# First stage of a one-core AdaLN block: matmuls whose products nobody reads, twelve direct fills, and q stored by three transfers

## The chip, the cores and the metric

The kernel runs on one core of a Trainium2 chip. The core has TensorE (PE, with its weight loads shown apart as PEld), VectorE (DVE), ScalarE (ACT), GpSimd (POOL) and SyncE (SP), which here only issues transfers. ACT issues some transfers too. The metric is the device time of one execution in microseconds (us). Every engine works through its own list of instructions in order, and semaphores order the engines among each other.

## The reference

Eight batches of 512 tokens of 128 channels go through a block of attention with 16 heads of 8 channels and a mixture of experts. Weights of the attention are binarized (sign times the row's mean magnitude).

```python
mod = (silu(c) @ wmod).reshape(8, 6, 1, 128)          # sa, ca, ga, sb, cb, gb
h = layernorm(x) * (1 + ca) + sa
q, k, v = (split_heads(binlinear(h, W, b)) for W, b in ((Wq, bq), (Wk, bk), (Wv, bv)))
att = softmax(einsum('bhtd,bhsd->bhts', q, k) * 8 ** -0.5)
y = einsum('bhts,bhsd->bhtd', att, v)
x = x + ga * binlinear(merge(y), Wp, bp)
h = layernorm(x) * (1 + cb) + sb
x = x + gb * (shared_expert(h) + top_2_of_8_experts(h))
```

## The kernel before

**Batches and slots.** Attention goes through the eight batches in turn, and each batch through 16 slots: four groups of four heads, times four tiles of 128 keys. In a slot PE makes four score products (`st`, L1609), ACT takes their exponentials (L868), and PE multiplies them with v (`pv`, L1620). The softmax needs the largest score of each query first. For that, PE makes the scores a second time the other way round into a bank pair (`mx`, L1594), and DVE takes the maxima of the pair (`neg_max`, L1077). One such pair is called a fill: 32 fills a batch, numbered on through all batches, 8 a group of heads, made one after the other into two bank pairs. Fill f may start when the reduction of fill f-2 is over. Eleven fills (0 to 10) are made before the first slot of the first batch; its first five slots make three fills each and later slots two. When a group's eight fills are reduced, PE transposes the maxima (`max_T`, L1527), DVE splits them into two bf16 rows (`split_max`, L1085 and L1087), and two small transfers put them beside q.

**Stacks.** The fills and scores of L1594 and L1609 work on `qs` and `ks`, in which each head's 8 channels stand as three bf16 parts, stacked on 72 rows. The parts come from `first_part` (L429, DVE) and `split_qk` (L437 to L441), go to DRAM (`q_parts`, `k_parts`) and come back as stacks of a group of four heads, three transfers for q and three for k.

**Direct fills.** The first group cannot wait for that. `project_direct` (L1646) projects q and k of four heads onto strips of 32 partitions (into `st` and `pv`), ACT writes them to the space of `x1`, and the fills 0 to 7 are made from these in f32 (L1584). This is what `DIRECT = 1` says.

**Order before the first slot.** It is written out by hand for each engine. On PE: the modulation, the transposes of the normalised x of batch 0 (L1487), the bias on strips (L1637, after all small constants are there), the weights of q and k (L1628), q (L1514), k and q on strips, k, the fills, and between them the weights of v, v (L1520), x of batch 1, its q and its k. DVE does the statistics and normalisation (L1026 to L1034), cleans the weights, and splits q of batch 0 itself; POOL splits k. ACT evacuates all of these, and issues the stores of k, the first two groups of k stacks (L448) and the first maxima's transfers (L928). SP stores q of batch 0 by six transfers (three for the first four heads, three for the others), loads x of batch 2, loads the q stacks of groups 0 and 1, and then waits until group 1 and the first maxima are there before it loads groups 2 and 3.

**After the attention** come the experts (from about 590 us on), which the change leaves as they are.

## Time and profile before

| | us |
|---|---|
| runs of the kernel before | 667.86, 669.41, 663.66; median 667.86 |
| the profiled execution, its time | 667.02 |
| its span, first to last instruction | 665.2 |
| PE busy | 615.2 (92%) |
| DVE busy | 504.9 (76%) |
| ACT busy | 404.1 (61%) |
| POOL busy | 259.2 (39%) |

The busy share is an average. Over most of the attention PE has work all the time; in the first 60 us, where the change is, PE, DVE and ACT take turns in waiting. The granted clock of TensorE is its share of 2.4 GHz: 1.00 is 2.4 GHz, 0.50 is 1.2 GHz.

### The profile page before, as it was taken

The numbers are of one execution on the slowest core, as the hardware profiler recorded it, in microseconds if no ns is written. First come the engines' busy times: TensorE is split into PE (matmuls) and PEld (weight loads), VectorE is DVE, ScalarE is ACT, GpSimd is POOL, SyncE is SP. The second block draws the span as 40 slices with busy tenths as digits, with TensorE's granted clock in tenths as the row PEclk, the third lists the DMA queues.
The fourth block names the chain that finished last, engine by engine and source line by source line (L and its number), as shares of the span: only waits on it lengthen the run. The fifth ranks groups of instructions, "written<-read, shape, count | busy, mean of one in ns | idle before, by whom it ended". The sixth has DMA issues, their size and how long they took to land.

```text
span 665.2 us, 10688 instructions
## 1 busy us (share of the span) xinstructions
PE 615.2 (92%) x3461; PEld 288.7 (43%) x3461; DVE 504.9 (76%) x1065; ACT 404.1 (61%) x791; POOL 259.2 (39%) x309
## 2 busy tenths in 40 slices
PE   4899999999999999999999999999999589886997
PEld 2332324233333333423333333232378578776855
DVE  5779788889988989888998888988467534433567
ACT  2345777777777776777778778678735224433431
POOL 4240041414352451434336235025056656566610
PEclk9969999999999999999999999999999988997999
DMA  3443332442541445344244244214832223222155
GB/s 103 134 121 117 117 114 98 132 131 90 160 123 64 133 134 134 109 149 116 93 147 127 69 133 130 67 50 135 226 81 57 68 65 88 63 68 61 56 185 195
DMA packets 58828, 73.91 MB, mean 111 GB/s; under 512 B 10857, under 2 KB 39819, under 8 KB 58772
## 3 DMA queue, kind: packets, MB, share of 16 engines
q1 hardware_dynamic: 53144, 63.30, 32.0%
q0 software_dynamic: 4320, 8.47, 3.7%
q10 hardware_dynamic: 1308, 1.46, 0.8%
q8 instruction: 28, 0.46, 0.3%
q14 instruction: 28, 0.23, 0.1%
HBM read 38.36 MB, written 34.96 MB: 110 GB/s over the span
## 4 chain that ended last, share of the span: by engine, by line
PE 73%; DVE 12%; ACT 7%; issue 3%; another core or an unknown queue 2%; DMA 1%; SPq 1%; POOL 1%; ACTq 1%; DVEq 0%; POOLq 0%
PE pv L1620 15%; PE st L1609 15%; PE mx L1594 14%; PE mx L1806 7%; DVE neg_max L1077 6%; PE st L1820 5%; PE mx L1754 3%; PE misc L1487 2%; PE misc L1514 2%; PE st L1770 2%; ACT pt L868 2%; PE pv L1794 1%; PE misc L1520 1%; DVE stats_sb L1026 1%
## 5 line engine op out<-in xcount | busy, mean ns | idle before, releaser
L868 ACT ACTIVATE pt<-st 128x512 f32<-128x512 f32 x496 | 282.1, 598 | 105.8 <-PE st L1609 95.9
L1077 DVE TENSOR_REDUCE neg_max<-mx 128x2 f32<-128x1024 f32 x248 | 294.5, 1215 | 47.9 <-PE mx L1594 44.6
L1620 PE MATMUL pv<-pt,vs 128*32 128x512 f32 x1024 | 136.4, 605 | 0.3 <-ACT pt L868 0.3
L745 POOL DMA_INDIRECT routed<-rec,row_u x64 | 64.1, 1002 | 136.6 <-PE pv L1620 114.8
L812 POOL DMA_INDIRECT results<-qs,home_u x71 | 72.0, 1014 | 50.8 <-ACT qs L995 28.4
L1609 PE MATMUL st<-even_qk 74*128 74x512 bf16 x256 | 89.0, 389 | 1.9 <-ACT pt L868 1.1
L1609 PE MATMUL st<-qs,ks 74*128 74x512 bf16 x240 | 81.4, 383 | 1.8 <-ACT pt L868 1.1
L1594 PE MATMUL mx<-ks,qs 72*128 72x512 bf16 x256 | 76.5, 380 | 2.9 <-DVE neg_max L1077 2.5
L1594 PE MATMUL mx<-even_qk 72*128 72x512 bf16 x240 | 74.5, 393 | 4.4 <-DVE neg_max L1077 4.1
L437 POOL TENSOR_TENSOR qk_r<-qk_f,qk_parts 128x512 f32<-128x512 f32 x15 | 17.4, 1161 | 98.8 <-DVE qk_parts L429 98.7
L1609 PEld LDWEIGHTS st<-even_qk 74*128 74x128 bf16 x256 | 20.9, 99 | 71.5 <-ACT pt L868 51.7
L989 ACT ACTIVATE vs<-mx 128x512 f32<-128x512 f32 (+1 forms) x43 | 22.7, 527 | 43.8 <-PE mx L1806 20.9
L1609 PEld LDWEIGHTS st<-qs,ks 74*128 74x128 bf16 x240 | 18.8, 98 | 67.5 <-ACT pt L868 51.5
L1806 PE MATMUL mx<-vs,pt 128*128 128x256 f32 (+1 forms) x224 | 48.1, 361 | 0.0
L1370 DVE TENSOR_TENSOR vs<-vs,mx 128x512 f32<-128x512 f32 (+1 forms) x29 | 17.2, 591 | 36.8 <-ACT vs L989 34.4
L1620 PEld LDWEIGHTS pv<-pt,vs 128*32 128x32 f32 x1024 | 20.1, 108 | 52.9 <-issue 37.6
L995 ACT ACTIVATE qs<-st,ks 128x128 f32<-128x128 f32 x71 | 23.2, 370 | 32.2 <-PE st L1820 20.6
L1806 PEld LDWEIGHTS mx<-vs,pt 128*128 128x128 f32 x224 | 38.8, 208 | 3.4
L1594 PEld LDWEIGHTS mx<-even_qk 72*128 72x128 bf16 x240 | 22.2, 100 | 35.0 <-DVE neg_max L1077 13.0
L1594 PEld LDWEIGHTS mx<-ks,qs 72*128 72x128 bf16 x256 | 23.7, 98 | 31.4 <-DVE neg_max L1077 8.2
L1794 PE MATMUL pv<-ident,ks 128*128 128x128 f32 x71 | 15.7, 287 | 21.9 <-ACT vs L984 13.4
L1370 DVE TENSOR_TENSOR pt<-vs,mx 128x512 f32<-128x512 f32 (+1 forms) x14 | 8.3, 591 | 24.0 <-issue 23.5
(217 smaller groups left out, 798.0 us busy)
## 6 DMA issues: line engine op xcount, KB each, us to landing
routed<-pad_rows SPq DMA_DIRECT2D x64, 260.0 KB
even_qk<-q_parts SPq DMA_DIRECT2D x48, 96.0 KB
qs<-q_parts SPq DMA_DIRECT2D x48, 96.0 KB
ks<-k_parts SPq DMA_DIRECT2D x48, 96.0 KB
even_qk<-k_parts SPq DMA_DIRECT2D x42, 96.0 KB
ks<-routed SPq DMA_DIRECT2D x28, 130.0 KB
q_parts<-qk_parts SPq DMA_DIRECT2D x21, 128.0 KB
k_parts<-qk_parts SPq DMA_DIRECT2D x7, 384.0 KB, 2.3
```

Of the source, the lines that this page charges most:

```text
L745: pool.indirect_dma_start(out=routed_dram, out_offset=bass.IndirectOffsetOnAxis(ap=row_u[:, k, t:t + 1], axis=0), in_=rec[b.par][:, k, t, ...
L812: pool.indirect_dma_start(out=result_dram, out_offset=bass.IndirectOffsetOnAxis(ap=home_u[:, slot, h:h + 1], axis=0), in_=y_u[slot][:, h, ...
L868: act.activation(pt[n % 2][:, hh, :], score_bank(b, n, hh), ACT.Exp, scale=SCALE).then_inc(exp_done, 1)
L989: act.activation(silu_u[u % 2][:, 0:halves(u) * I], up_bank(u, 0), ACT.Silu).then_inc(silu_ready, 1)
L995: last = act.activation(y_u[u % RING][:, h, :], y_bank(u)[:, h, :], ACT.Copy, scale=xu[u % RING][:, h, C:C + 1])
L1077: dve.tensor_reduce(neg_max[g % 2][:, hh, 2 * half:2 * half + 2], mx_bank[half][:], AX_X, ALU.max, negate=True).then_inc(mx_free, 1)
L1370: dve.tensor_tensor(act_u[u % ARING][:, 0:halves(u) * I], silu_u[u % 2][:, 0:halves(u) * I], up_bank(u, 1), ALU.mult).then_inc(act_ready, 1)
L1594: last = pe.matmul(mx_bank[half][:, t, :], qs[b.par][0:PROD, h, q0:q0 + P], ks[b.par][0:PROD, h, :], start=True, stop=True)
L1609: pe.matmul(score_bank(b, n, hh), ks[b.par][0:STACK, h, j * P:(j + 1) * P], qs[b.par][0:STACK, h, :], start=True, stop=True).then_inc(st_f ...
L1620: last = pe.matmul(pv_bank[32 * hh:32 * (hh + 1), :], vs[b.par][:, j, HG * g + hh, :], pt[n % 2][:, hh, :], start=(n % Y_SLOTS == 0), stop ...
L1806: last = pe.matmul(up_bank(u, m // IC)[:, m % IC * rows:(m % IC + 1) * rows], w_unit[u % WRING][:, m * P:(m + 1) * P], xuT[u % 2][:, 0:row ...
L1820: last = pe.matmul(y_bank(u)[:, h, :], act_u[u % ARING][:, first:first + P], w_unit[u % WRING][:, 2 * I + j * C:2 * I + (j + 1) * C], star ...
```

## The change

1. **Unread products.** `keep_busy(n)` issues n matmuls of 128x512 in bf16 from a block of ones into `mx` bank pair 1; nobody reads the result. There are 20 of them on PE ahead of the first strips: 7 at the start, then 5, 4, 2 and 2 between the real steps. DVE sets the ones (one memset).
2. **Loads at the start.** bq and bk come right after Wq and Wk, and have a semaphore of their own, on which the bias on strips now waits; bv, bp, the router's bias and the shared weights come after x of batch 1, whose load is issued as soon as x of batch 0 is normalised.
3. **Twelve direct fills.** The second group of heads is put on strips too (`DIRECT = 2`), and fills 8 to 11 are made from these.
4. **Order.** k and q on strips now stand ahead of q and k. DVE takes k's first part after fill 0, and does no split any more; POOL splits q and k of batch 0, and its constants come after that. The normalisation of batch 1 stands behind the maxima of the first group, and with it batch 1's transposes, q and k on PE. ACT stores k after v is evacuated, issues only the first group's k stack, and issues the first maxima's transfers ahead of batch 1's evacuations; the ones for the k stacks are loaded later.
5. **q stored by three transfers** for all 16 heads; the q and k stacks of groups 1, 2 and 3 follow on SP with no wait for the first maxima, and x of batch 2 is loaded behind group 2.

```diff
-DIRECT = 1
-DIRECT_FILLS = DIRECT * 2 * HG
+DIRECT = 2
+DIRECT_FILLS = 3 * HG
...
+        busy_ops = scratch[1][:, 0:T // 2]
...
-            load_x(B1)
             sp.wait_ge(parts_ready, 1)
-            store_q_heads(0, HG, first_stored[0])
-            store_q_heads(HG, H, q_stored)
-            load_x(B1.plus(1))
-            sp.wait_ge(first_stored[0], 16 * PARTS)
+            store_q_heads(0, H, q_stored)
             load_q_stack(B0, 0)
-            load_q_stack(B0, 1)
-            sp.wait_ge(stack_loaded[0][1], STACK_DMAS)
-            sp.wait_ge(m_row_loaded[0], ROW_DMAS)
-            for g in (2, 3):
+            for g in (1, 2, 3):
                 load_stack(B0, g)
+                if g == 2:
+                    load_x(B1.plus(1))
...
             first_part(dve, B0, 0, use(AHEAD, "q_0"))
-            split_qk(dve, B0, 0)
+            maxima(range(1))
+            first_part(dve, B0, 1, use(AHEAD, "k_0"))
+
+            maxima(range(1, 2 * HG))
+            split_max(B0, 0, use(AHEAD, "m0"))
             layer_norm1(B1)
-            first_part(dve, B0, 1, use(AHEAD, "k_0"))
-
-            maxima(range(DIRECT_FILLS))
-            split_max(B0, 0, use(AHEAD, "m0"))
-            maxima(range(DIRECT_FILLS, FIRST_FILLS))
+            maxima(range(2 * HG, FIRST_FILLS))
...
+            def keep_busy(count):
+
+                ones = busy_ops.bitcast(BF16)
+                for _ in range(count):
+                    pe.matmul(mx_bank[1][:, 1, :], ones[:, 0:P], ones, start=True, stop=True)
+
+            pe.wait_ge(busy_ready, 1)
+            keep_busy(7)
...
+            keep_busy(4)
             ln1_T(B0, use(AHEAD, "ln1_0"))
             spread_bias()
+            keep_busy(2)
             weights_T(0)
-            pe.wait_ge(first_done, 2)
+            keep_busy(2)
+            free(use(AHEAD, "q_0"))
+            project_direct(1, 0, 2)
+            project_direct(0, 0, 2)
             project(0, use(AHEAD, "q_0"))
-            project_direct(1, 0, 1)
-            project_direct(0, 0, 2)
             project(1, use(AHEAD, "k_0"))
...
                 if fill == 5:
+                    project_direct(1, 1, 4)
+                    project_direct(0, 1, 4)
+                if fill == 2 * HG - 1:
+                    max_T(B0, 0, use(AHEAD, "m0"))
+                if fill == 2 * HG:
                     ln1_T(B1, use(AHEAD, "ln1_1"))
-                if fill == DIRECT_FILLS - 1:
+                if fill == 2 * HG + 1:
                     project(0, use(AHEAD, "q_1"))
-                    max_T(B0, 0, use(AHEAD, "m0"))
             project(1, use(AHEAD, "k_1"))
```

**PE, from batch 0's transposes to the first fill, before** (a name's number is that of its bank; x1 is the space of the strips):

```order
L1487 MATMUL misc<-ident,ln1 128x128 x4
L1637 MATMUL st1<-bias_qkv,ident 32x2 x4
L1628 MATMUL st0<-ident,w_nat 128x128 x2
L1514 MATMUL misc<-hT,wT 128x512
L1646 MATMUL st1<-hT,wT 32x512 x4
L1646 MATMUL pv<-hT,wT 32x512 x4
L1514 MATMUL misc<-hT,wT 128x512
L1584 MATMUL mx0<-x1 128x512 x2
```

The same stretch of PE after, with the unread products at L1504:

```order
L1504 MATMUL mx1<-pt1 128x512 x4
L1492 MATMUL misc<-ident,ln1 128x128 x4
L1651 MATMUL st1<-bias_qkv,ident 32x2 x8
L1504 MATMUL mx1<-pt1 128x512 x2
L1642 MATMUL st0<-ident,w_nat 128x128 x2
L1504 MATMUL mx1<-pt1 128x512 x2
L1660 MATMUL st1<-hT,wT 32x512 x4
L1660 MATMUL pv<-hT,wT 32x512 x4
L1528 MATMUL misc<-hT,wT 128x512 x2
L1598 MATMUL mx0<-x1 128x512 x2
```

The strips (32x512) moved ahead of the projection of q, and k's projection follows q's at once; eight unread products stand between the real steps.

PE from fill 7 to the first scores, before; L1487 of batch 1 stands ahead of this piece, between the fills 5 and 6:

```order
L1584 MATMUL mx1<-x1 128x512 x2
L1514 MATMUL misc<-hT,wT 128x512
L1527 MATMUL misc<-ident,neg_max0 16x128
L1594 MATMUL mx0<-even_qk 128x512 x2
L1594 MATMUL mx1<-even_qk 128x512 x2
L1594 MATMUL mx0<-even_qk 128x512 x2
L1514 MATMUL misc<-hT,wT 128x512
L1609 MATMUL st0<-even_qk 128x512
```

PE from fill 5 to the first scores, after (L1660 is the second group's strips, L1541 the transpose of the maxima):

```order
L1598 MATMUL mx1<-x1 128x512 x2
L1660 MATMUL st1<-hT,wT 32x512 x4
L1660 MATMUL pv<-hT,wT 32x512 x4
L1598 MATMUL mx0<-x1 128x512 x2
L1598 MATMUL mx1<-x1 128x512 x2
L1541 MATMUL misc<-ident,neg_max0 16x128
L1598 MATMUL mx0<-x1 128x512 x2
L1492 MATMUL misc<-ident,ln1 128x128 x4
L1598 MATMUL mx1<-x1 128x512 x2
L1528 MATMUL misc<-hT,wT 128x512
L1598 MATMUL mx0<-x1 128x512 x2
L1528 MATMUL misc<-hT,wT 128x512
```

All of batch 1's first work (L1492, L1528) now stands behind the transpose of the maxima, and so behind the reduction of fill 7, and the fills 8 to 10 are f32 fills of the strips in place of bf16 fills of the stacks.

DVE from q's first part to fill 10, before (L1074 and L1077 are the reductions):

```order
L429 CAST qk_parts<-qk_f 128x512
L437 TENSOR_TENSOR qk_r<-qk_f,qk_parts 128x512
L439 CAST qk_parts<-qk_r 128x512
L441 TENSOR_TENSOR qk_parts<-qk_r,qk_parts 128x512
L1034 TENSOR_SCALAR ln<-x_in,mv,rstd 128x128 x4
L429 CAST qk_parts<-qk_f 128x512
L1074 TENSOR_REDUCE neg_max<-mx 128x2 x8
L1085 CAST m_rows<-misc 16x128
L1087 TENSOR_TENSOR m_rows<-misc,m_rows 16x128
L1077 TENSOR_REDUCE neg_max<-mx 128x2 x3
```

The same stretch after:

```order
L432 CAST qk_parts<-qk_f 128x512
L1078 TENSOR_REDUCE neg_max<-mx 128x2
L432 CAST qk_parts<-qk_f 128x512
L1078 TENSOR_REDUCE neg_max<-mx 128x2 x7
L1089 CAST m_rows<-misc 16x128
L1091 TENSOR_TENSOR m_rows<-misc,m_rows 16x128
L1038 TENSOR_SCALAR ln<-x_in,mv,rstd 128x128 x4
```

The three split instructions went to POOL, k's first part now stands behind fill 0, and the normalisation moved from ahead of the fills to behind the split of the maxima, ahead of fill 8.

## Rows read from the trace of the kernel before

**Rows 1.** Head of the page.
```profile
span 665.2 us, 10688 instructions
```
**Rows 2.** Windows: stretch, length, engines' busy time, PEclk (granted clock), DMA share, GB/s.
```profile
17.40:27.00 9.60, 9.49 (x46) 4.15 (x44) 7.38 (x10) 4.03 (x7) 4.87 (x6) 1.00 0.49 146
27.00:31.00 4.00, 2.76 (x10) 0.60 (x6) 3.08 (x3) 0.78 (x1) 0.00 (x0) 1.00 0.70 192
31.00:37.40 6.40, 5.16 (x10) 1.48 (x10) 4.13 (x5) 0.69 (x1) 0.00 (x0) 0.50 0.09 21
37.40:44.70 7.30, 7.30 (x23) 3.70 (x21) 4.16 (x5) 3.88 (x8) 3.31 (x4) 0.50 0.52 153
44.70:60.00 15.30, 13.98 (x69) 3.50 (x71) 14.05 (x24) 9.11 (x17) 3.89 (x5) 1.00 0.47 143
...
601.40:604.70 3.30, 3.30 (x17) 3.30 (x18) 1.77 (x6) 1.41 (x6) 2.60 (x3) 0.53 0.18 56
```
**Rows 3.** Timeline of PE: start us, length us, line, form, count, [idle before, releaser].
```profile
10.45 0.28 PE L1637 MATMUL st<-bias_qkv,ident 128*32 128x2 f32 x8 [1.17 <-DMA router_bias<-L_ffn_routing_bias]
...
11.83 2.08 PE L1514 MATMUL misc<-hT,wT 128*128 128x512 f32 x2 [0.47 <-ACT wT L893]
13.83 1.94 PE L1646 MATMUL st<-hT,wT 128*32 128x512 f32 x8
...
17.40 1.12 PE L1514 MATMUL misc<-hT,wT 128*128 128x512 f32 x2
18.46 1.99 PE L1584 MATMUL mx<-x 32*128 32x512 f32 x8
...
23.11 1.16 PE L1520 MATMUL misc<-wT,hT 128*128 128x128 f32 x8
...
30.15 1.23 PE L1514 MATMUL misc<-hT,wT 128*128 128x512 f32 x2 [1.24 <-ACT hT L845]
...
37.40 1.06 PE L1609 MATMUL st<-even_qk 74*128 74x512 bf16 x2
...
41.67 1.92 PE L1520 MATMUL misc<-wT,hT 128*128 128x128 f32 x8
```
**Rows 4.** Timeline of DVE, the same columns.
```profile
16.97 1.11 DVE L1034 TENSOR_SCALAR ln<-x_in,mv,rstd 128x128 f32<-128x128 f32 x4
19.29 0.43 DVE L429 CAST qk_parts<-qk_f 128x512 bf16<-128x512 f32 x1 [1.20 <-ACT qk_f L853]
19.63 4.81 DVE L1074 TENSOR_REDUCE neg_max<-mx 128x2 f32<-128x1024 f32 x4
25.37 4.86 DVE L1074 TENSOR_REDUCE neg_max<-mx 128x2 f32<-128x1024 f32 x4 [0.92 <-PE mx L1584]
32.58 0.28 DVE L1085 CAST m_rows<-misc 16x128 bf16<-16x128 f32 x1 [2.35 <-PE misc L1527]
...
33.58 3.58 DVE L1077 TENSOR_REDUCE neg_max<-mx 128x2 f32<-128x1024 f32 x3 [0.42 <-PE mx L1594]
39.35 1.22 DVE L1077 TENSOR_REDUCE neg_max<-mx 128x2 f32<-128x1024 f32 x1 [2.19 <-PE mx L1594]
...
45.10 1.22 DVE L1077 TENSOR_REDUCE neg_max<-mx 128x2 f32<-128x1024 f32 x1 [1.59 <-PE mx L1594]
```
**Rows 5.** Timeline of ACT, and the transfers that it issues (ACTq).
```profile
25.69 3.58 ACTq L448 DMA_DIRECT2D even_qk<-k_parts  x6
29.32 0.78 ACT L845 ACTIVATE hT<-misc,mod_T 128x512 f32<-128x512 f32 x1 [4.27 <-issue]
```
**Rows 6.** Timeline of SP's issues: a q stack of one group, and batch 1's q store.
```profile
39.63 2.20 SPq L525 DMA_DIRECT2D even_qk<-q_parts  x3
...
44.29 2.01 SPq L508 DMA_DIRECT2D q_parts<-qk_parts  x3
```
**Rows 7.** Timeline of POOL: the first and the last of k's three split instructions.
```profile
19.79 1.15 POOL L437 TENSOR_TENSOR qk_r<-qk_f,qk_parts 128x512 f32<-128x512 f32 x1 [4.10 <-DVE qk_parts L429]
...
21.81 1.15 POOL L441 TENSOR_TENSOR qk_parts<-qk_r,qk_parts 128x512 bf16<-128x512 f32 x1
```

More of the change, by code:

```diff
@@ L213, in adaln_block @@
         strips_ready = sem("strips_ready")
-        first_stored = [sem(f"first_stored{i}") for i in range(2)]
+        busy_ready = sem("busy_ready")
+        first_stored = sem("first_stored")
         small_loaded = sem("small_loaded")
+        qk_bias_loaded = sem("qk_bias_loaded")
         c_loaded = sem("c_loaded")
@@ L425, in first_part @@
                 dve.wait_ge((q_stored, k_stored)[i], all_stored(b.plus(-1), i))
-            if b.const == 1:
-                dve.wait_ge(first_stored[i], 16 * (PARTS, 1)[i])
+            if b.const == 1 and i == 1:
+                dve.wait_ge(first_stored, 16)
             dve.wait_ge(misc_free, done + 1)
@@ L443, in load_k_stack @@
         def load_k_stack(eng, b, g):
-            eng.wait_ge(*((first_stored[1], 16) if b.const == 0 and g == 0 else (k_stored, all_stored(b, 1))))
+            eng.wait_ge(*((first_stored, 16) if b.const == 0 and g == 0 else (k_stored, all_stored(b, 1))))
             for j in range(PARTS):
@@ L769, in scatter @@
                     scatter_rows(b, i)
+            split_qk(pool, B0, 0)
+            split_qk(pool, B0, 1)
+            rstd(mv1, ve1, var1_ready, rstd1, rstd1_ready, stats1_ready, B1)
+            pool.affine_select(out=earlier_token[:], in_=ones_bf[:], compare_op=ALU.is_gt, fill=0.0, base=0,
+                               pattern=[[1, P]], channel_multiplier=-1).then_inc(consts_ready, 1)
+            pool.memset(marks[:], 0.0).then_inc(consts_ready, 1)
+            pool.sem_inc(rows_free, 2)
+            pool.iota(expert_no[:], pattern=[[1, E]], base=0, channel_multiplier=0,
+                      allow_small_or_imprecise_dtypes=True).then_inc(consts_ready, 1)
+            pool.iota(next_row[0][:], pattern=[[REGION, E]], base=0, channel_multiplier=0,
+                      allow_small_or_imprecise_dtypes=True).then_inc(consts_ready, 1)
+            for k in range(RING):
+                pool.memset(digit[:, k:k + 1], float(E ** k)).then_inc(consts_ready, 1)
+            pool.memset(pad_rows[:], 0.0).then_inc(pad_ready, 1)
+            pool.wait_ge(pad_ready, 1)
+            pool.memset(pad_rows[:, :, C + 1], float(FAR)).then_inc(pad_ready, 1)
+            pool.iota(first_row[:], pattern=[[REGION, E]], base=0, channel_multiplier=0,
+                      allow_small_or_imprecise_dtypes=True).then_inc(consts_ready, 1)
+            pool.iota(unit_start[:], pattern=[[P, 2 * EARLY_PAIRS]], base=0, channel_multiplier=0,
+                      allow_small_or_imprecise_dtypes=True).then_inc(consts_ready, 1)
+            pool.affine_select(out=earlier[:], in_=ones_bf[:, 0:E * E].rearrange("p (e f) -> p e f", e=E), compare_op=ALU.is_gt,
+                               fill=0.0, base=0, pattern=[[1, E], [-1, E]], channel_multiplier=0).then_inc(consts_ready, 1)
+            pool.iota(home[:], pattern=[[TOKENS, K_TOP], [1, TT]], base=0, channel_multiplier=TT,
+                      allow_small_or_imprecise_dtypes=True).then_inc(setup_pool, 1)
             pool.wait_ge(setup_pool, 4)
-            rstd(mv1, ve1, var1_ready, rstd1, rstd1_ready, stats1_ready, B1)
-            split_qk(pool, B0, 1)
             fill_values(pool, 1)
@@ L828, in _ @@
             act.dma_start(wmod_sb[:], wmod).then_inc(wmod_loaded, 16)
-            act.wait_ge(setup_pool, 3)
-            for i in range(2):
-                load_ones(act, i)
             act.wait_ge(misc_full, use(AHEAD, "c") + 1)
@@ L1587, in max_scores @@
                     return
-                if hh == 0 and half == 0:
+                if hh == 0 and half == 0 or fill == DIRECT_FILLS:
                     pe.wait_ge(stack_loaded[b.par][g], STACK_DMAS * (b.half + 1))
```

70 lines of the change are left out of this document (29 added, 41 removed).

## The prediction

> **What bounds the kernel now.** I read the head of the page first, then the windows of the first 60 us, then the timelines of PE and DVE there, and last ACT, SP and POOL. The span is 665.2 us [rows 1], of an execution of 667.02 us; the median of the runs is 667.86. From 44.7 us on PE is busy 13.98 of 15.30 us and DVE 14.05 [rows 2]: from there the kernel is a full line that the change does not touch. So what counts is how much earlier that line starts. As its marker I take the end of fill 14's reduction, 45.10 + 1.22 = 46.32 us [rows 4]: it closes the last long wait of DVE, and every later fill, slot and batch follows it.
>
> Up to the marker DVE does 15 reductions of 1.2 us, and waits between them: 0.92 us ahead of fill 4, 2.35 ahead of the split of the maxima, then 0.42, 2.19 and 1.59 [rows 4]. PE runs at half clock twice. Until about 17.4 us a 512-column f32 projection takes 2.08 us, and at 17.40 it takes 1.12 [rows 3] (the clock column reads 1.00 there, since nothing is recorded ahead of its first change; the durations tell). After 31.0 us the granted clock is 0.50, that is 1.2 GHz, up to 44.7 [rows 2]. Ahead of that fall PE idled 1.24 us [rows 3] and was busy only 2.76 of 4 us [rows 2]. The idling came from ACT, which issued six transfers for 3.58 us before it evacuated batch 1's transposes [rows 5].
>
> **The start.** The bias on strips waited 1.17 us for the last small constant [rows 3], and that wait goes, since bq and bk come early. The unread products keep PE busy from about 1 us, so that the real work from 9 us on should be at 2.4 GHz. The eight behind batch 0's modulation are in its path, but at some 0.27 us each (two bf16 products of 512 columns take 1.06 us at 1.2 GHz [rows 3], so half of half of that at full clock), 2.1 us in all, they fit in while DVE normalises x and cleans the weights; at half clock they would cost up to 2 us of their own. I put the first strip at 10.9 us, where PE's first projection was at 11.83.
> From there, warm: k's and q's strips 0.95 each (half of 1.94), q's projection 1.1, ACT's three evacuations at 0.78 or less [rows 5] ending at 14.65, k's projection to 15.8, fill 0 another 1.0 (half of 1.99 for two) [rows 3]. Fill 0's reduction starts at 16.95, where it was 19.63 [rows 4]: **2.7 us earlier**.
>
> **Fills 1 to 7.** DVE drops q's split, but takes k's first part (0.43) behind fill 0. Fill 3, v (1.16) and fills 4 and 5 fill PE up to 23.9; then come the second group's strips, 2 x 0.95 us of new PE work ahead of fill 6. DVE must wait for fill 4 (0.9 us) and for fill 6 (1.4 us). Fill 7 is reduced at 29.35, where it was 30.23: of the 2.7 us only **0.9** are left.
>
> **Fills 8 to 10 and batch 1.** The transpose of the maxima stands ahead of fill 8, so PE idles from 27.8 to 29.4; then fill 8, and PE idles again, 30.8 to 31.6, while DVE splits the maxima (0.6) and normalises batch 1 (1.11) [rows 4]. Behind that PE has batch 1's transposes, fill 9, q, fill 10, k without a break. Everything now hangs on the clock there.
> Warm: transposes 0.6, fill 1.0, q 1.1, fill 1.0, k 1.1 bring the first score to 36.4 us (it was 37.40). Slot 0 then has three fills, the first f32, and v (1.16); DVE does two first parts (0.75); the chain of reductions 11 to 14 ends at 43.55: **-2.8 us** at the marker.
> With the clock lost at about 30.5 and back at about 36.5: fill 9 takes 1.75 and q 1.7, the rest as before; first score 38.3, marker 45.4: **-0.9 us**.
> With the clock lost and not back: fills 9, 10 and 11 take 1.75 each, q, k and v 1.7 to 1.9 [rows 3]; first score 39.55, marker 49.45: **+3.1 us**. The f32 fills cost here: at half clock each takes 1.75 us (twice a warm one, less its overlap), where the two bf16 products that it replaces take at most 1.06 [rows 3].
>
> **Which of the three.** The row of before has a fall after one gap of 1.24 us beside work that left PE idle 1.24 of 4 us. I forecast gaps of 1.6 and 0.8 in the same 4 us, so I expect the fall. As to the return: before, it took up to 44.7 us, the last 7.3 of them with PE busy all the time [rows 2], of mostly bf16 products on 72 rows; but at the start it came in 5.6 us of f32 work (11.83 to 17.40), and late in the kernel a stretch of f32 work from 601.40 was back at full clock by 604.70 [rows 2, 3]. What stands behind 31.6 us is all f32, so I take 5 us.
> The Trainium skill (TensorE: Matmul & The Clock Gate, HAM oscillation) puts the loss of the clock down to waits of PE that outlast a whole window of its monitor, and my gaps would not do that: by that rule the warm sum of -2.8 holds. This case's trace does not agree, since the clock fell beside a gap of 1.24 us.
>
> **Edits that cost nothing.** POOL splits q before k: q from 15.2, k from 18.6, at 3.2 us each (19.79 to 22.96) [rows 7], so q's parts are there at 18.4 and k's at 21.8 (22.96 before). q's store issues 2.0 us, each q stack 2.2 [rows 6]; with 3 us assumed for a landing, which no row here gives, group 0's stack is there at about 28, and group 0's k stack, issued by ACT behind the second strips at 26.6, at 31: over 5 us ahead of the first score. Uncovered, each would cost its lateness one to one. The first maxima's two transfers go out at 30.4 and have 6 us, but now run beside the stacks of groups 2 and 3, which before waited for them; below nothing I see no gain, above I allow 1 us. x of batch 2 is now loaded at some 33 us and used in slot 1, past 41. Batch 1's evacuation waited 4.27 us behind ACT's issues [rows 5] and no longer does; that gain is already spent, since batch 1's x is normalised later than it was evacuated.
>
> **The rivals.**
> 1. *The clock falls and comes back* near 36.5: -0.9 us, 666.96. Chance 0.46.
> 2. *The clock holds* through both gaps (the rule above): -2.8 us, 665.1. For it: DVE's reductions may start earlier than I have them, and the gaps shrink. Against: the fall of before. Chance 0.25.
> 3. *Slower: f32 fills at half clock.* The clock falls near 30 us and is not back when slot 0's v is projected: +3.1 us, 671.0. It decides from a return later than about 40 us on. Slots of 72-row products without f32 work speak for it, five f32 steps in a row against it. Chance 0.13.
> 4. *The unread products do not raise the clock* ahead of the strips: then k's and q's strips and q's projection take 5.0 us in place of 3.0, and the first reduction starts at about 19.05; 2.1 us are missing all the way, +1.2 us, 669.1. For it: the products are followed by waits for loads and the normalisation. Chance 0.07.
> 5. *Something larger*: all of DVE's waits before the marker (0.92 + 2.35 + 0.42 + 2.19 + 1.59, 7.5 us in all) vanish, which with the start 2.7 earlier, less the normalisation and first part that now stand among them (1.5), would be -8.7 us; or a stack or the maxima land late. Chance 0.09, about evenly.
>
> **How the numbers follow.** The likeliest gives 667.86 - 0.9 = 667.0. Its own range is 665.5 to 669. Rivals 2, 3 and 4 lie at 665.1, 671.0 and 669.1; the runs of before lie up to 4 us from each other's median, so I take 662.0 to 670.8. A change of 1% (6.7 us) is about what a measurement of this kernel can tell from none. Only rival 5 reaches that on the fast side, with 0.06 to 0.07, and on the slow side it and a bad case of rival 3, with 0.05: faster 0.07, same 0.88, slower 0.05.
>
> **What would show it.** In the changed profile: the first strip near 10.9 us, with an f32 projection of 1.1 us from the start (step 1; 2.1 us means rival 4); the first reduction near 17 us; fill 7's near 28.2; two gaps of PE between 27.8 and 31.6; first score between 36.4 and 39.6; fill 14's reduction over by 43.6, 45.4 or 49.5 for rivals 2, 1 and 3, with the granted clock of 28 to 45 us to tell them apart. The difference of this marker should be the difference of the times. If the marker moves by one amount and the span by another, the step that is wrong is that the line behind it is full. If PE waits for a DMA at the first score, the covers were wrong.

## The result and the profile after

The changed kernel takes 674.01 us (median of 11 runs, 667.0 to 676.1) and the kernel before 665.49 (11 runs, 663.3 to 669.4): a ratio of 1.0099, with a 95% interval of 1.0064 to 1.0135. It is **slower by 1.0%**. I had forecast 667.0 and a range of 662.0 to 670.8, with 0.05 on slower by over 1%. The profiled execution took 674.29 us.

The head of its page, of which the first line answers [rows 1]: the span, the busy time of PE, and the granted clock in 40 slices.

```profile
span 672.5 us, 10793 instructions
PE 630.4 (94%) x3513; PEld 293.9 (44%) x3513; DVE 502.3 (75%) x1063; ACT 405.9 (60%) x793; POOL 261.8 (39%) x312
PEclk9659999999999999999999999999999978997999
```

The span is 7.3 us longer, and PE is busy 15 us more (it was 615.2): 20 unread products and the second group's strips were added, and, as the next rows show, more of its work ran at half clock. In the clock row two slices near the start are low (6 and 5). The windows of the first 60 us, in the columns of [rows 2]:

```profile
12.00:17.00 5.00, 4.22 (x17) 1.38 (x14) 1.27 (x2) 2.29 (x4) 2.33 (x3) 1.00 0.05 16
17.00:19.00 2.00, 1.47 (x6) 0.40 (x6) 2.00 (x4) 1.60 (x2) 1.64 (x2) 1.00 0.08 18
19.00:29.00 10.00, 9.94 (x32) 3.99 (x36) 4.81 (x5) 1.24 (x5) 7.03 (x26) 0.51 0.49 141
29.00:33.00 4.00, 2.86 (x16) 0.68 (x8) 1.95 (x2) 1.27 (x2) 0.00 (x0) 0.93 0.63 169
33.00:37.00 4.00, 3.44 (x11) 1.40 (x11) 3.00 (x8) 0.00 (x0) 0.00 (x0) 0.50 0.58 128
37.00:44.80 7.80, 7.80 (x12) 2.07 (x13) 2.66 (x3) 1.46 (x2) 0.00 (x0) 0.50 0.38 110
44.80:53.30 8.50, 8.50 (x24) 3.78 (x23) 4.16 (x5) 3.81 (x8) 3.34 (x4) 0.50 0.00 1
53.30:60.00 6.70, 5.69 (x30) 1.35 (x28) 6.23 (x15) 4.16 (x8) 3.87 (x5) 1.00 0.37 120
```

The clock is lost **twice**: from about 19.2 to 29.3 us, and from 32.8 to 53.3. That is 30.6 us recorded at 1.2 GHz, where before it was 13.7 (31.0 to 44.7), besides the stretch up to 17.4 us that only the durations of [rows 3] give away. From 37 to 53.3 PE works without a break, 16.3 of 16.3 us, and stays at half clock.

PE's timeline (start, duration, line, operation and count, and in brackets the idle time ahead), to be read against [rows 3]. Line numbers have moved: L1598 is L1584 of before (f32 fills), L1660 is L1646 (strips), L1528 is L1514, L1534 is L1520 (v), L1541 is L1527, L1623 is L1609 (scores).

```profile
10.17 1.06 PE L1660 MATMUL st<-hT,wT 128*32 128x512 f32 x8
12.03 1.12 PE L1528 MATMUL misc<-hT,wT 128*128 128x512 f32 x2
17.44 1.13 PE L1598 MATMUL mx<-x 32*128 32x512 f32 x4
19.06 2.00 PE L1598 MATMUL mx<-x 32*128 32x512 f32 x4 [0.49 <-DVE neg_max L1078]
20.99 2.08 PE L1534 MATMUL misc<-wT,hT 128*128 128x128 f32 x8
23.00 3.79 PE L1598 MATMUL mx<-x 32*128 32x512 f32 x8
26.71 1.94 PE L1660 MATMUL st<-hT,wT 128*32 128x512 f32 x8
...
33.56 0.37 PE L1541 MATMUL misc<-ident,neg_max 128*16 128x128 f32 x1 [1.69 <-DVE neg_max L1078]
33.86 2.08 PE L1598 MATMUL mx<-x 32*128 32x512 f32 x4
...
38.92 2.08 PE L1528 MATMUL misc<-hT,wT 128*128 128x512 f32 x2
...
44.80 1.06 PE L1623 MATMUL st<-even_qk 74*128 74x512 bf16 x2
```

The start is as forecast: strips at 10.17, a projection in 1.12 us. But a fill that took 1.13 us at 17.44 takes 2.00 at 19.06, behind a gap of only 0.49 (PE had been busy 5.69 of the 7 us before 19.00). Up to 29 us the f32 work then takes about twice its time. The second gap (1.69 us) is the forecast one, and behind it each f32 fill and projection occupies 2.0 us (38.92 less the start of the fill before it, 36.91). The first score starts at 44.80; it was 37.40.

DVE's timeline, against [rows 4] (L1078 is L1074 of before, L1081 is L1077):

```profile
16.16 1.23 DVE L1078 TENSOR_REDUCE neg_max<-mx 128x2 f32<-128x1024 f32 x1 [1.82 <-PE mx L1598]
...
25.12 1.23 DVE L1078 TENSOR_REDUCE neg_max<-mx 128x2 f32<-128x1024 f32 x1 [2.79 <-PE mx L1598]
...
31.05 2.36 DVE L1078 TENSOR_REDUCE neg_max<-mx 128x2 f32<-128x1024 f32 x2 [3.00 <-PE mx L1598]
...
47.92 1.23 DVE L1078 TENSOR_REDUCE neg_max<-mx 128x2 f32<-128x1024 f32 x1 [3.64 <-PE mx L1598]
...
53.73 1.22 DVE L1081 TENSOR_REDUCE neg_max<-mx 128x2 f32<-128x1024 f32 x1 [1.66 <-PE mx L1608]
```

The last row is fill 14's reduction: **the marker is at 54.95**, 8.6 us later than 46.32. The waits are all for PE, none for a transfer. That the line behind the marker is full, as the prediction held, is seen in the last exponentials of the attention, on ACT's timeline of before and then of after:

```profile
475.13 1.08 ACT L868 ACTIVATE pt<-st 128x512 f32<-128x512 f32 x2
```

```profile
483.53 1.09 ACT L868 ACTIVATE pt<-st 128x512 f32<-128x512 f32 x2
```

From marker to here are 428.8 us before and 428.6 after. The attention ends 8.4 us later; the experts gave back 1.1 of it in this execution, which leaves the 7.3 of the span.

### The profile page after: what moved, and what is told of

It is laid out like the page before. It is cut to its first block, busy times and chain, and to the rows that moved or that the text cites. A ratio compares the mean times of both kernels' runs of the same rounds, so it can differ in the third digit from the quotient of the medians.

```text
span 672.5 us, 10793 instructions
## 1 busy us (share of the span) xinstructions
PE 630.4 (94%) x3513; PEld 293.9 (44%) x3513; DVE 502.3 (75%) x1063; ACT 405.9 (60%) x793; POOL 261.8 (39%) x312
## 4 chain that ended last, share of the span: by engine, by line
PE 75%; DVE 11%; ACT 6%; another core or an unknown queue 3%; issue 2%; DMA 1%; POOL 0%; ACTq 0%; DVEq 0%; POOLq 0%
PE pv L1634 15%; PE st L1623 15%; PE mx L1608 13%; PE mx L1827 7%; DVE neg_max L1081 6%; PE st L1841 5%; PE misc L1492 3%; PE mx L1775 3%; PE misc L1528 2%; PE mx L1598 2%; PE st L1791 2%; ACT pt L868 2%; PE misc L1534 2%; PE pv L1815 1%
## 5 line engine op out<-in xcount | busy, mean ns | idle before, releaser
L1081 DVE TENSOR_REDUCE neg_max<-mx 128x2 f32<-128x1024 f32 x244 | 289.7, 1215 | 45.8 <-PE mx L1608 43.1
L1623 PE MATMUL st<-even_qk 74*128 74x512 bf16 x256 | 89.0, 389 | 1.9 <-ACT pt L868 1.1
L1623 PE MATMUL st<-qs,ks 74*128 74x512 bf16 x240 | 81.4, 383 | 1.8 <-ACT pt L868 1.1
L1608 PE MATMUL mx<-even_qk 72*128 72x512 bf16 x232 | 70.5, 385 | 3.9 <-DVE neg_max L1081 3.6
L1623 PEld LDWEIGHTS st<-even_qk 74*128 74x128 bf16 x256 | 20.9, 99 | 72.6 <-ACT pt L868 51.3
L1623 PEld LDWEIGHTS st<-qs,ks 74*128 74x128 bf16 x240 | 18.8, 98 | 67.5 <-ACT pt L868 51.5
L1078 DVE TENSOR_REDUCE neg_max<-mx 128x2 f32<-128x1024 f32 x12 | 14.5, 1223 | 17.7 <-PE mx L1598 17.7
```

What stands on the lines that cost most here:

```text
L1081: dve.tensor_reduce(neg_max[g % 2][:, hh, 2 * half:2 * half + 2], mx_bank[half][:], AX_X, ALU.max, negate=True).then_inc(mx_free, 1)
L1608: last = pe.matmul(mx_bank[half][:, t, :], qs[b.par][0:PROD, h, q0:q0 + P], ks[b.par][0:PROD, h, :], start=True, stop=True)
L1623: pe.matmul(score_bank(b, n, hh), ks[b.par][0:STACK, h, j * P:(j + 1) * P], qs[b.par][0:STACK, h, :], start=True, stop=True).then_inc(st_f ...
```

## The experiments

All went by the same two marks, marker and last exponentials, and by a ratio to the kernel before on the same chip. The chips differ (the kernel before takes 642 us on two of them, 666 and 669 on others), so only ratios are compared. I give them with the 95% interval. Marker and last exponentials are of one execution of each kernel, the profiled one; the ratio is of all its runs, and the two need not match one for one. Every run also has its mean granted clock, and where the runs of one kernel differ in it I say so.

| kernel | marker | last exponentials | ratio |
|---|---|---|---|
| before | 46.32 | 475.13 | 1 |
| changed | 54.95 | 483.53 | 1.0099 [1.0064, 1.0135] |
| a_nobusy | 52.14 | 484.31 | 1.0149 [1.0116, 1.0183] |
| d_first_hold | 49.94 | 478.47 | 1.0075 [1.0038, 1.0113] |
| d_second_hold | 47.46 | 476.49 | 0.9986 [0.9957, 1.0016] |
| a_fillers | 42.84 | 471.85 | 0.9968 [0.9954, 0.9981] |
| a_direct1 | 45.83 | 474.68 | 1.0019 [0.9997, 1.0041] |
| d_direct1_fillers | 45.14 | 474.78 | 1.0014 [0.9996, 1.0033] |
| a_early | 46.61 | 486.89 | 1.0017 [0.9967, 1.0068] |
| a_early_fillers | 46.97 | 477.85 | 1.0002 [0.9970, 1.0033] |
| b_busy | 43.92 | 473.25 | 0.9974 [0.9954, 0.9994] |
| b_stores | 49.90 | 478.45 | 1.0044 [1.0018, 1.0069] |
| b_stores_fillers | 47.64 | 476.63 | 1.0008 [0.9989, 1.0028] |
| b_fillers | 42.23 | 471.15 | 0.9934 [0.9908, 0.9961] |
| b_busy_fillers | 46.56 | 475.82 | 0.9936 [0.9910, 0.9963] |
| b_fill_dense | 42.51 | 471.89 | 0.9966 [0.9945, 0.9988] |
| c_dense | 40.73 | 469.32 | 0.9913 [0.9886, 0.9940] |

Names with a_ and d_ are made from the changed kernel, b_ and c_ from the one before. "Products" below are unread ones, as in part 1 of the change.

**Does the order lose, or the clock?** a_fillers is the changed kernel with thirteen more products, at the two places where its clock falls.

```diff
+                if fill == 2:
+                    keep_busy(4, pv_bank)
                 if fill == 2 * HG - 1:
+                    keep_busy(6, st_bank[0])
                     max_T(B0, 0, use(AHEAD, "m0"))
                 if fill == 2 * HG:
+                    keep_busy(3, st_bank[0])
                     ln1_T(B1, use(AHEAD, "ln1_1"))
```

> The changed kernel with 13 more unread products in TensorE's waits: 4 behind fill 2, 6 ahead of the transpose of the maxima, 3 ahead of batch 1's transposes; at full clock 2.8 us of work, placed where TensorE stood still. Theory C (half clock is the loss): the clock holds or comes back soon, the fill 14 reduction ends at 43 to 45 us in place of 54.95 (before: 46.32), the time is 0.993 to 0.998 of before. Rival O (the order is the loss: second group's strips, f32 fills, batch 1's work behind the maxima, whatever the clock): the clock holds and the time is still 1.005 or more. If the clock falls all the same, the run tells nothing between them.

Its windows, and the reductions of fills 12 to 14:

```profile
17.00:27.00 10.00, 9.74 (x53) 3.79 (x54) 7.16 (x8) 4.12 (x7) 8.71 (x27) 1.00 0.43 121
27.00:31.00 4.00, 3.66 (x15) 1.10 (x14) 3.51 (x9) 0.00 (x0) 0.00 (x0) 1.00 0.77 188
31.00:37.00 6.00, 6.00 (x23) 2.11 (x22) 3.60 (x4) 2.42 (x4) 0.00 (x0) 1.00 0.85 214
```

```profile
39.36 3.48 DVE L1081 TENSOR_REDUCE neg_max<-mx 128x2 f32<-128x1024 f32 x3
```

The clock is 1.00 throughout, the marker is at 39.36 + 3.48 = 42.84 (the warm sum of the prediction had 43.55), and the kernel is 0.3% faster than the one before. So thirteen products take 12.1 us off the marker and 1.3% off the ratio. All twelve runs have a mean granted clock of 0.999 or 1.000 and lie within 1.4 us. It is the lost clock that makes the change slower than the kernel before, and not the order and the added f32 work. (That these cost something at full clock too is seen at c_dense, below.)

**Which of the two losses?** Two kernels keep the products at one place only. d_first_hold has of this diff just the four behind fill 2, and d_second_hold the six and three around `max_T`, without the four.

> The changed kernel with only the four unread products behind fill 2. It shares the clock's loss between its two places: in the changed kernel TensorE was at half clock from 19.2 to 29.3 us and again from 32.8 to 53.3 us, fill 7 was reduced at 33.4 us and fill 14 at 54.95; with products at both places these were 28.95 and 42.84. Theory (the second loss carries most): the first is gone, fill 7 is reduced near 29 us, the clock falls behind that at the wait for the maxima and stays low, fill 14 is reduced near 50.5 us (54.95 less 4.4), ratio to the kernel before 1.002 to 1.008 (changed kernel: 1.0099). Rival (one loss brings the other: the second happened because the first had set DVE and PE out of step): the clock holds, fill 14 near 43 us, ratio near 0.997.

> The changed kernel with only the nine unread products around the first transpose of maxima (six ahead of it, three ahead of batch 1's transposes). Theory (the second loss carries most): the fall near 19 us and the return near 29 stay, fill 7 is reduced near 33.4 us, the clock then holds, fill 14 is reduced near 47.3 us (42.84 + 4.4), ratio 1.002 to 1.005. Rival: the nine products arrive too early or at half clock, cost up to 1.9 us more (9 x 0.21), and the clock falls at 33 us all the same: fill 14 near 55 to 57 us, ratio 1.010 to 1.014.

The windows of d_first_hold:

```profile
19.00:29.00 10.00, 8.46 (x47) 3.15 (x45) 7.16 (x7) 2.60 (x6) 7.13 (x26) 1.00 0.55 146
29.00:33.00 4.00, 3.11 (x11) 1.61 (x13) 2.72 (x8) 0.66 (x1) 0.00 (x0) 0.74 0.81 165
33.00:37.00 4.00, 4.00 (x8) 1.00 (x6) 1.23 (x1) 0.76 (x2) 0.00 (x0) 0.50 0.88 215
```

And of d_second_hold:

```profile
19.00:29.00 10.00, 9.80 (x32) 3.86 (x36) 4.96 (x5) 1.64 (x5) 7.19 (x26) 0.54 0.51 139
33.00:37.00 4.00, 3.71 (x18) 1.31 (x16) 3.27 (x8) 0.56 (x1) 0.00 (x0) 1.00 0.65 122
```

Each place holds the clock for itself alone: the second loss comes without the first (d_first_hold), and the first without the second (d_second_hold). Without the first the marker is at 49.94, 5.0 us earlier; without the second at 47.46, 7.5 earlier; 5.0 + 7.5 = 12.5, against 12.1 with both. Marker and expectation agree within 0.6 us in both. The ratio of d_first_hold is as expected (1.0075, in 1.002 to 1.008); that of d_second_hold is better (0.9986 where 1.002 to 1.005 was expected).

The clocks of its ten runs tell why: **the first loss comes in some executions only**. Four runs have a mean granted clock of 0.999 to 1.000 and take 637.3 to 639.4 us, so they were at half clock for a microsecond or so at most; five have 0.991 to 0.994 and take 641.6 to 644.1 (the last one has 0.983 and 648.0). The profiled execution is of the second kind (0.991, 643.8). The means of the four and the five are 638.6 and 643.2: 4.5 us apart, near the 5.0 that the first loss costs at the marker, and the five alone stand at 1.002 of the kernel before (642.0), as expected. The second loss shows no such choice in d_first_hold: all its five runs have 0.981 to 0.987.

d_first_hold is also the prediction's rival 3 as a kernel: one loss behind fill 7, not back at v. That rival had the marker at 49.45. In d_first_hold the clock fell near 30.9 us and was back near 48.0.

**The unread products at the start.** a_nobusy is the changed kernel without its 20 products (`keep_busy(7)`, 5, 4, 2 and 2 taken out).

> The changed kernel without its 20 unread products; everything else as changed. Changed against before is 1.010. Theory C (the loss is TensorE time at half clock between 19 and 53 us, and the products only help ahead of it): the strips and projections before 17 us run at half clock again, the first reduction (16.16 us in the changed kernel) comes at 18 to 19 us, and the time is 1.010 to 1.015 of before. Rival P (the products do harm: they bring the clock up early, so that it is taken back early, at 19 us): without them the clock rises near 17 us and lasts to about 30 as in the kernel before, and the time is 1.000 to 1.006.

```profile
31.00:50.00 19.00, 19.00 (x43) 6.93 (x44) 9.31 (x14) 5.05 (x10) 3.12 (x4) 0.50 0.45 92
50.00:60.00 10.00, 10.00 (x32) 2.64 (x33) 7.33 (x16) 4.39 (x8) 4.09 (x5) 0.50 0.25 80
60.00:70.00 10.00, 9.72 (x47) 2.15 (x44) 7.58 (x12) 5.02 (x9) 0.00 (x0) 0.92 0.62 194
```

The first reduction starts at 18.09, not 16.16, so the products are worth 1.9 us there. There is no loss near 19 us in this execution, behind the same gap of 0.49 us; but the one behind fill 7 lasts past 60 us, with PE busy all 29 us from 31 to 60. The marker, at 52.14, does not hold all of that; the last exponentials (+9.2) do.

b_busy puts the same 20 products, and the loads at the start (part 2), into the kernel before.

> The kernel before with only the 20 unread products and the new order of the loads at the start (biases of q and k early, x of batch 1 ahead of the others). Theory C: projections and strips at full clock from the start, first reduction at 16.5 to 17.5 us in place of 19.63; 1 to 3 us faster, 0.996 to 0.999. Rival P (an early clock is taken back early, and the f32 fills between 19 and 29 us run at half clock): first reduction as early, but fill 7's no earlier than the 30.2 us of before, and 1.000 to 1.008.

Its first reductions start at 16.15 (before 19.63) and its marker is at 43.92. Of the 3.5 us gained 2.4 are left: fill 8 waits 1.06 us for the second group's k stack. Its clock falls all the same and is low for as long as in the kernel before (13.6 us from 28.5 on, against 13.7). Ratio 0.9974: parts 1 and 2 alone are a small gain.

**The second group's f32 work.** a_direct1 sets `DIRECT = 1` and eight direct fills in the changed kernel, and drops the second strips; d_direct1_fillers does so with the thirteen products.

```diff
-DIRECT = 2
-DIRECT_FILLS = 3 * HG
+DIRECT = 1
+DIRECT_FILLS = 2 * HG
...
-                if fill == 5:
-                    project_direct(1, 1, 4)
-                    project_direct(0, 1, 4)
```

> The changed kernel with DIRECT = 1 again: no strips of the second group (4 f32 projections onto strips and two evacuations less), and the fills 8 to 11 are bf16 products of the stacks. All else as changed. At the half clock of the changed kernel's trace the strips took 3.4 us and each f32 fill 2.0 us where a bf16 fill takes 0.85. Theory F (the f32 work of the second group is the loss): 3.4 + 4 x 1.15 = 8 us less, the fill 14 reduction ends at 46 to 48 us, the time is 0.998 to 1.002 of before. Rival G (the place of batch 1's work and the waits around the maxima are the loss): at least 4 us stay, 1.006 or more.

> The changed kernel with all thirteen further unread products, and with eight direct fills in place of twelve (no strips of the second group). It asks what the second group's f32 work costs when the clock is held: it is two strips of 1.0 us, and four fills of 1.0 in place of 0.6, 3.6 us of PE. Theory (the strips cover the second group's k stack, which is late behind one store of q for all heads): fill 8 waits over 2 us for that stack, PE falls idle there, and nothing is won: ratio 0.997 to 1.003 against 0.9968 with twelve. Rival (the f32 work lies in the path): fill 14 is reduced 2 to 3.6 us earlier than 42.84, ratio 0.991 to 0.994.

PE's timeline of a_direct1 at fill 3 and at fill 8, then of d_direct1_fillers at fill 8, and the latter's windows behind it:

```profile
19.02 1.13 PE L1596 MATMUL mx<-x 32*128 32x512 f32 x4 [0.49 <-DVE neg_max L1076]
...
32.57 1.03 PE L1606 MATMUL mx<-even_qk 72*128 72x512 bf16 x2 [4.38 <-DMA even_qk<-k_parts]
```

```profile
31.87 1.04 PE L1606 MATMUL mx<-even_qk 72*128 72x512 bf16 x2 [3.72 <-DMA even_qk<-k_parts]
```

```profile
32.00:35.00 3.00, 3.00 (x10) 1.63 (x10) 1.23 (x1) 0.00 (x0) 0.00 (x0) 0.50 0.71 201
35.00:36.00 1.00, 0.65 (x4) 0.09 (x1) 0.40 (x1) 0.78 (x1) 0.00 (x0) 0.96 0.70 203
```

Without the strips, fill 8 waits 4 us for a stack, and behind that wait the clock is at 0.50 from 31.7 to 35.1 us even with the thirteen products; the ten runs have mean clocks of 0.992 to 0.997 where a_fillers has 0.999 to 1.000. With the products, that version is worse than a_fillers (marker 45.14 against 42.84, ratio 1.0014 against 0.9968), by the wait and by the clock that goes with it; what each of the two takes was not parted. Without them it is better than the changed kernel (1.0019 against 1.0099). There it has less f32 work at half clock, and its profiled execution kept the clock at fill 3, behind the same gap of 0.49 us and, from the first strips on, the same instructions, and had it at 0.50 from 25.2 to 38.9 only. So beside the late stack of parts 4 and 5, part 3 pays its way while the clock is held and costs when it is lost.

**Part 5, the stores and stacks.** b_stores is the kernel before with only part 5; b_stores_fillers adds the 15 products of b_fillers, below.

```diff
-            store_q_heads(0, HG, first_stored[0])
-            store_q_heads(HG, H, q_stored)
-            load_x(B1.plus(1))
-            sp.wait_ge(first_stored[0], 16 * PARTS)
+            store_q_heads(0, H, q_stored)
...
-            sp.wait_ge(stack_loaded[0][1], STACK_DMAS)
-            sp.wait_ge(m_row_loaded[0], ROW_DMAS)
             for g in (2, 3):
                 load_stack(B0, g)
+                if g == 2:
+                    load_x(B1.plus(1))
```

> The kernel before with only q's store by three transfers for all heads, the q and k stacks of the groups 2 and 3 with no wait for the first maxima, and x of batch 2 behind group 2. Theory H (hidden): first group's stack is there in time, 0.999 to 1.001. Rival T (the stacks of groups 2 and 3 delay the first maxima's small transfers or the second group's k stack on the shared queues): first score or fill 8 waits for a DMA, 1.002 or more.

> b_stores (1.0044; TensorE waited 2.60 us for the k stack of the second group ahead of fill 8) with the 15 products of b_fillers in the waits. Theory T (the late stack is a wait of its own, whatever the clock): the clock holds or comes back soon, but fill 8 still waits 2 to 4 us for the stack; b_fillers (0.9934) plus 3 us, 0.996 to 1.000. Rival (b_stores lost only by the clock that its wait cost): as b_fillers, 0.992 to 0.995.

```profile
36.34 1.89 PE L1590 MATMUL mx<-even_qk 72*128 72x512 bf16 x4 [2.60 <-DMA even_qk<-k_parts]
```

```profile
36.64 1.39 PE L1601 MATMUL mx<-even_qk 72*128 72x512 bf16 x4 [2.95 <-DMA even_qk<-k_parts]
```

In both, fill 8 waits for the second group's k stack, 2.6 and 2.95 us. Against the kernel before, the marker is 3.6 and 1.3 us late; against b_fillers (42.23), which has the same products, b_stores_fillers is 5.4 us late, and its clock was at 0.50 from 37.2 to 40.4 us behind the wait. Part 5 is not free by itself; in the changed kernel fills 8 to 11 do not need that stack, and the wait is covered. I had put this edit at nothing for the right reason, and had named its price uncovered only as "its lateness one to one", with no number.

**Batch 1 where it was.** a_early is the changed kernel with batch 1's normalisation, transposes and q back among the fills, ahead of the transpose of the maxima; a_early_fillers adds ten products.

> The changed kernel with batch 1's first work put back among the first fills: POOL makes batch 1's rstd ahead of the splits, DVE normalises batch 1 ahead of fill 0, TensorE transposes it behind fill 6 and projects its q behind fill 7, ahead of the transpose of the maxima. Strips of the second group and f32 fills stay. Theory C+O: TensorE's wait ahead of the transpose of the maxima is filled with real work (1.7 us of waiting at 32 us in the changed kernel), the 1.1 us of normalisation leave DVE's chain; if the clock falls at 19 us all the same, the time is 1.003 to 1.007; if it holds, 0.995 to 0.999. Rival F (the f32 work of the second group sets the loss whenever the clock is low): 1.006 or more.

> The changed kernel with batch 1's work back among the fills (as a_early, 1.0017, whose trace lost the clock at 32 us and did not have it back at 60) and 10 more unread products (1, 2 and 1 behind the fills 1, 2 and 4, 4 ahead of the transpose of the maxima, 2 behind fill 9). Theory C: with the clock held both of a_fillers' and a_early's gains are there: first score at 33 to 34.5 us, fill 14's reduction over at 40 to 41.5, time 0.989 to 0.993. Rival O (strips and f32 fills of the second group bound it): no better than a_fillers, 0.996 to 0.998.

a_early has runs from 664 to 684 us and its ratio decides nothing; its profiled execution is one of the long ones (681.4), so I read only the start of it. The clock falls near 32 us there too. a_early_fillers held it up to 36.8, but then:

```profile
36.66 0.96 PE L1623 MATMUL st<-even_qk 74*128 74x512 bf16 x2 [1.39 <-DMA even_qk<-m_rows]
```

The first score waits 1.39 us for the first maxima, two small transfers among the stacks, and the clock is lost there (back near 50.4 us). I expected 0.989 to 0.993 and got 1.0002. Its runs go from 661.4 us at a mean clock of 0.995 to 673.0 at 0.971, so not every execution loses as much. The wait is the risk of 0 to 1 us that I allowed for the first maxima's transfers, a little larger; it shows when PE arrives early.

**The same cure in the kernel before.** b_fillers puts 15 products between fill 7 and fill 10 of the kernel before; b_busy_fillers is b_busy with them; c_dense adds one product behind each of the fills 1, 2, 4 and 6 to that (the diff's first two lines), and b_fill_dense adds these four to b_fillers.

```diff
+                if fill in (1, 2, 4, 6):
+                    keep_busy(1, pv_bank)
                 if fill == DIRECT_FILLS - 1:
+                    keep_busy(6, st_bank[0])
                     project(0, use(AHEAD, "q_1"))
+                    keep_busy(3, st_bank[0])
                     max_T(B0, 0, use(AHEAD, "m0"))
+                    keep_busy(3, st_bank[0])
+                if fill == DIRECT_FILLS + 1:
+                    keep_busy(3, st_bank[0])
```

> The kernel before with 15 unread products in the waits between fill 7 and fill 10 (6, 3, 3, 3) and nothing else of the change. In its trace the clock fell at 31.0 us and came back at 44.7. Theory C: it holds, the fill 14 reduction ends at 43.5 to 44.5 us in place of 46.32, the time is 0.995 to 0.998. Rival D (there DVE's chain sets the pace, TensorE's clock is hidden): 0.999 to 1.002 with the clock full.

> The kernel before with the 20 unread products and the new order of the loads at the start, and the same 15 in the later waits. Theory C: the gains of b_busy (0.9974) and of a full clock between 28 and 43 us add up: fill 14's reduction over at 40 to 42 us, the time is 0.990 to 0.995, better than a_fillers (0.9968), since no strips of a second group and no f32 fills 8 to 11 stand in the way. Rival S (the next thing late is the k stack of the second group, which TensorE already waited for in b_busy): fill 8 waits 1 to 3 us for it, and 0.996 to 0.999.

> b_fillers (0.9934) with the same four products behind the fills 1, 2, 4 and 6; no products before the first fill, loads at the start as before. Here the clock held already, so the four add nothing but their 0.2 us each in waits of DVE's pace: 0.992 to 0.995, fill 14's reduction over at 42 to 43 us. If products behind each fill delay DVE's chain (each 0.22 us where TensorE's slack a fill is 0.2), 0.995 to 0.997.

> b_busy_fillers with four more unread products, one behind each of the fills 1, 2, 4 and 6 (before, with the 20 products, the new loads at the start, 19 products in later waits). b_busy_fillers' trace lost the clock at 19.0 us, when the first f32 fills ran with short waits between them, and had it back at 36; its fill 14 reduction ended at 46.6 us and its time was 0.9936. Theory C (the unread products must go on through the fills): the clock holds from 5 us on, the fill 14 reduction ends at 39.5 to 41 us, the time is 0.986 to 0.991. Rival: one product in 1.2 us is too little, the clock falls near 19 us as often, 0.992 to 0.995.

DVE in b_fillers, the reductions of fills 8 to 14, beside waits of 0.42, 2.19 and 1.59 us in [rows 4]:

```profile
33.29 3.49 DVE L1080 TENSOR_REDUCE neg_max<-mx 128x2 f32<-128x1024 f32 x3 [0.64 <-PE mx L1605]
36.94 1.23 DVE L1080 TENSOR_REDUCE neg_max<-mx 128x2 f32<-128x1024 f32 x1 [0.16 <-PE mx L1605]
38.75 3.48 DVE L1080 TENSOR_REDUCE neg_max<-mx 128x2 f32<-128x1024 f32 x3
```

With the clock held, the marker of b_fillers is 4.1 us earlier, and the kernel before becomes 0.7% faster (0.9934) by fifteen products that nobody reads. Of the 4.1, 0.7 is there before any of them: the first reduction stands at 18.96 where the trace of before has 19.63, a difference between two executions. So some 3.4 us are theirs. b_busy_fillers has the same ratio over its runs, but its profiled execution, the slowest of the twelve, lost the clock at 19 us, as the changed kernel did, with the marker back at 46.56. That led to c_dense, with its price of a product beside each reduction:

```profile
23.56 1.23 DVE L1081 TENSOR_REDUCE neg_max<-mx 128x2 f32<-128x1024 f32 x1 [0.15 <-PE mx L1601]
...
37.25 3.48 DVE L1084 TENSOR_REDUCE neg_max<-mx 128x2 f32<-128x1024 f32 x3
```

Its clock is 1.00 all through the first 60 us, DVE waits 0.15 us ahead of the fills 3, 5 and 7, and the marker is at 40.73. The ratio 0.9913 [0.9886, 0.9940] is the lowest of all, though b_fillers' and b_busy_fillers' intervals overlap it; **this version beats both kernels**. b_fill_dense, without the start's products, gains nothing from the four: its marker is 0.3 us behind that of b_fillers, and its 0.9966 against 0.9934 is no clear difference, since the intervals overlap.

c_dense also prices the rest of the change. It and a_fillers both have parts 1 and 2 and a clock of 1.00 through the first 60 us; a_fillers has parts 3 to 5 besides. Its marker is 2.1 us later (42.84 against 40.73) and its ratio 0.9968 [0.9954, 0.9981], clear of 0.9913. So at full clock the twelve direct fills, the new order and the new stores together cost some 2 us against the old order with held clock; which of them does was not parted.

## Why the prediction was wrong, step by step

- **The start: right.** First strip 10.17 (10.9 forecast), f32 projection 1.12 us, first reduction 16.16 (16.95). Rival 4 is out. Without the products it is 18.09.
- **Fills 1 to 7: right at full clock, wrong as it came.** DVE's waits ahead of fills 4 and 6 were to be 0.9 and 1.4 us, and are 0.92 and 1.41 in d_first_hold, where fill 7 is reduced at 29.00 (29.35 forecast). In the changed kernel it is 33.41. **The first failed step** is that I asked for the clock only from 27.8 us on. I had raised it at the start by dense bf16 products, and took for granted that the f32 fills behind would keep it. In the profiled execution it was lost at 19.2, and that costs 5.0 us at the marker.
- **The gaps and the second fall: right.** 1.6 and 0.8 us forecast; 1.69 and 0.74 in d_first_hold, and the clock falls.
- **The return: wrong, and the second failed step.** I took 5 us of f32 work from two stretches elsewhere ([rows 3] at the start, [rows 2] at 601 us). It took 20.5 us, and some 17 in d_first_hold, where nothing was lost before. The row that pointed the other way was in my own hands: [rows 2] had the last 7.3 us of the old loss with PE busy throughout at 0.50. I set it aside because its products were bf16 on 72 rows; here PE was busy with f32 fills and projections, and it lasted longer.
- **The size of rival 3: nearly right.** d_first_hold, which is that case, has its marker at 49.94 where the sum gave 49.45. Its f32 fills at half clock take 2.0 us each and not 1.75: no overlap is gained, which is more than the 0.5, and an earlier start (batch 1's transposes at 31.21 where I had 31.6) takes part of it back. Its chance, 0.13, was far too small, and my range ended at 670.8, below that rival's own 671.0. The double loss had no place in my list but the 0.09 for something larger.
- **The sum of the miss.** The marker was forecast 0.9 us early and came 8.6 late, 9.5 apart: 4.5 are the late return (d_first_hold stands at +3.6) and 5.0 the first loss.
- **The warm sum: right, as a kernel that was not the changed one.** -2.8 us forecast for the marker; a_fillers has -3.5, 13 more products and all. First score 36.4 forecast, 35.85 there. Its time gained less than its marker (0.3%, 2.1 us on that chip).
- **The line behind the marker is full: right.** In thirteen of the seventeen kernels the last exponentials stand 428.5 to 429.4 us behind the marker. The others are d_direct1_fillers (429.6) and a_nobusy, a_early and a_early_fillers (430.9 to 440.3), where the clock was lost or still low behind the marker or close to it. One correction to the text ahead: the attention ends near 480 us, and the experts follow from there.
- **Edits at nothing: right in the changed kernel.** No transfer is waited for at the first score. Part 5's price uncovered is a wait of 2.6 us and 3.6 us at the marker (b_stores).

Five of the eleven runs of the changed kernel lie from 667.0 to 670.4 us and six from 674.0 to 676.1. The distance is about the 5.0 us that the first loss costs, and the profiled execution, which has both losses, is of the upper group. The lower ones have mean granted clocks of 0.970 to 0.974 and the upper ones of 0.958 to 0.970; the two means, 0.9724 and 0.9648, differ by as much as 10.2 us at half clock would make over 672 us, and the first loss lasted 10.1. That the lower runs kept the clock through the first fills fits this, and d_second_hold, where four of ten runs did. No trace shows one of them, and on this chip the clock also varies in the experts, so for the changed kernel it is likely but not shown. In the lower runs, 667.0 to 670.4 us, the time is within my range; the median is of the others. What makes one execution lose the clock at 19 us and another not, of the same instructions up to there, stays open (besides the runs of d_second_hold: the changed kernel did and a_direct1 did not; b_busy_fillers did and b_busy did not).

## What to carry to other kernels

When a change adds f32 or narrow products to a stretch with short waits, price every step of that stretch at both clocks and take the slow one as a case of its own, from its first wait on; do not assume a return because PE is busy. If a few unread dense products at the waits take the loss away at 0.15 us each, try them before reordering anything: here they were worth 0.6 to 0.7% to the old order (b_fillers against before, c_dense against b_busy) and 1.3% to the new. And let them stand at every wait of the stretch, since each place holds only its own part (d_first_hold, d_second_hold). Last, read the mean granted clock of every run and not of the profiled one alone: a loss can come in some executions and not in others.

## What the hardware did that I had not expected

- **Half clock beside a busy PE.** In a_nobusy PE was busy 29.00 of 29 us (31 to 60 us) at a granted 0.50, on f32 fills, f32 projections and bf16 products on 72 rows; in the changed kernel 16.3 of 16.3 us. The Trainium skill (TensorE: Matmul & The Clock Gate, HAM oscillation) ties the loss to waits that outlast a window of the monitor. A gap of 0.49 us, at 19.06, is no such wait, and these unbroken stretches have no wait at all; here the measurement decides.
- **A fall behind a gap of 0.49 us**, between f32 fills on 32 rows. Four bf16 products of 128x512 at that place (d_first_hold, a_fillers) kept the clock at 1.00 in the next 10 us. The gap alone does not bring the fall: a_direct1 and a_nobusy have the same 0.49 us at the same place and the fill behind it takes 1.13 us.
- **The chips differ by 24 to 27 us in the kernel before, not at the start.** On the faster ones the last exponentials of a_fillers or d_second_hold stand as far behind the marker as on the others (429.0 us), so the difference lies in the experts. The clock is lower there on the slower chips (between 475 and 590 us 0.96 in before and in b_fillers, against 1.00 in a_fillers and d_second_hold). Whether that is the cause or comes of longer waits, no run here shows.
